# A decoder layer whose opening part is put in another order: weights and x turned first, one ternary form made by GpSimd, keys and values ahead of x1

## The chip, the cores and the metric

The kernel runs on one core of a Trainium2 chip, in one launch. The metric is the device time of that core in microseconds (us). In the text PE is TensorE, DVE is VectorE, ACT is ScalarE, POOL is GpSimd, SP is SyncE, which here only issues DMAs.

## The reference, cut to what matters

One post-norm decoder layer on 16 sequences of 256 tokens with 128 features, in three sub-layers, each followed by a residual sum and a layer norm.

```python
def bitlinear(x, weight):                       # weights made ternary
    scale = clip(mean(abs(weight), axis=1), 1e-05)
    w_q = clip(round(weight / scale), -1, 1)
    return x @ (weight + (w_q * scale - weight)).T

# 1: gated linear recurrence -> x1
r = sigmoid(bitlinear(x, Wr)); k = bitlinear(x, Wk); v = bitlinear(x, Wv)
scale = exp(positions * log(sigmoid(decay)))
state = cumsum(k * v / clip(scale, 1e-10)) * scale
x1 = layernorm(x + bitlinear(rmsnorm(r * state, ln_w), Wo))
# 2: cross attention, 16 heads of 64, over 1601 keys of ctx -> x2
q = x1 @ Wq + bq; k = ctx @ Wk + bk; v = ctx @ Wv + bv
x2 = layernorm(x1 + softmax(q k^T / 8) v @ Wo + bo)
# 3: top-1 mixture of 8 experts with capacity 512 -> output
x3 = layernorm(x2 + moe(x2))
```

## The kernel before, in words

Each engine has an instruction stream written out by hand, and semaphores tie the streams together. The attention goes by sequences ("batches" b, 16 of them) and within one by pairs of heads ("slots" s, 8 of them), 128 pairs in all. For each pair PE makes the keys (`keys`, lines 1406 to 1411, four pieces of 400 columns), the queries (`queries`, 1413), for every two pairs the values (`values`, 1424 to 1433, seven fills, 39 matmuls), then the row maxima of the scores (`maximum`, 1435, which DVE reduces at line 1048), the scores (`score_unit`), their sum with the exponentials from ACT (`attend`, 1473) and the denominators. Operands of keys, queries and values are split in a high part (`_hi`) and a low part (`_lo`), and each product is three matmuls, such as 1409, 1410 and 1411.

PSUM is a ring of eight banks. `all_fills` lists every fill of the ring in the order in which PE makes it, with the engine that empties it; all streams take bank numbers and semaphore counts from that list, so the list and the streams are changed together.

The recurrent sub-layer is done for two sequences at a time (a "step"). Step 0 stands in the prologue, ahead of the first batch. Its stages are: `step_tokens` (PE turns x), `step_rkv` (PE makes r, k and v with the ternary weights), `key_value`, `state`, `gated` (DVE, the chain that ends in `gain`), `step_products` (PE: the output product o and the sums of squares ss), `mean_square` (DVE), a power on POOL, `residual` and `step_moments` (DVE), another power on POOL, `normed` (DVE, writes `x1_rows`), `step_x1` (PE turns x1), and then high and low parts of x1, queries of pair 0 and its 16 maxima. From the maxima the `row_shift` of pair 0 goes through DRAM by SP's DMAs (`turn_shift`, 488 to 501) and comes back as `shift` (ACT, line 789); the first score matmul waits for it.

Before step 0 can start, DVE makes the ternary forms of four weights (lines 922 to 933), then the decay tables (936 to 948: a scan, a reciprocal, copies, memsets). PE in the meantime turns the context (`context`, line 1367), then the four ternary weights (`turn_weights`, 1344) and x. ACT copies three turned weights to `w_T`; DVE writes the fourth, scaled by ln_w (line 952), at the end of its tables, and `step_rkv` waits for it. POOL makes the low parts `wk_lo` (593) and `wv_lo` (605).

The staged copies of the projection weights (`wq_rows`, `wk_rows`, `wv_rows`) and the buffers of the ternary work lie in `v_sb`, which later holds the values, in two halves of 3328 columns per partition: the values of pairs 0 and 1 go in the first half. In the rows below all of these show as `v_sb`.

The order of PE in the prologue before is:

```python
for c in range(4): context(at, 0, c)
turn_weights(); step_tokens(at, 0)
pe.wait_ge(setup_ev_act, 1); pe.wait_ge(setup_ev_dve, 1)
step_rkv(at, 0); step_products(at, 0); context_read(at, 0)
pe.wait_ge(wk_split, 1)
for c in range(4): keys(at, 0, c)
step_x1(at, 0); pe.wait_ge(wq_split, 2); queries(at, 0)
# 16 maxima of pair 0, then seven value fills, keys and queries of pair 1, the bias row bo
```

Of the kernel before, what the change touches and what calls it, by code (L numbers as in the profile page):

```python
# [5 lines left out]
P = 128  # L6
F32 = mybir.dt.float32
# [3 lines left out]
ALU = mybir.AluOpType  # L11
ACT = mybir.ActivationFunctionType
# [20 lines left out]
V_FILLS = 7  # L33
# [38 lines left out]
def all_fills(batches):  # L72
# [3 lines left out]
    put = lambda owner, *key: fills.append((key, owner))  # L76
# [4 lines left out]

    for c in range(4):
        put("dve", "ctx", 0, c)
    step(0, "xt", "r", "kk", "vv", "o", "ss")
    for c in range(4):
        put("dve", "k", 0, c)
    step(0, "x1t")
# [4 lines left out]
    for n in range(V_FILLS):  # L92
        put("act", "v", 0, n)
# [105 lines left out]
def decoder_layer(nc, x, ctx, Wr, Wk, Wv, Wo, decay, ln_w, xWq, xbq, xWk, xbk, xWv, xbv, xWo, xbo,  # L199
                  fWr, fW1, fW2, out):  # L200
    B, T, D = x.shape
# [40 lines left out]
    with ExitStack() as stack:  # L242
# [3 lines left out]
        def sem(name):  # L246
            return stack.enter_context(nc.semaphore(name))
# [103 lines left out]
        wq_rows, wk_rows, wv_rows = (spare[:, n * AD:(n + 1) * AD] for n in range(3))  # L351
        w_rows, w_tmp, w_tern = (spare[:, 3 * AD + n * 4 * P:3 * AD + (n + 1) * 4 * P].rearrange("p (m n) -> p m n", n=P)
# [214 lines left out]
        def _(pool):  # L567
# [146 lines left out]
        def _(act):  # L714
# [202 lines left out]
        def _(dve):  # L917
# [7 lines left out]
            own(v.tensor_scalar(w_nhalf[:, :], w_scale[:, :], -0.5, None, ALU.mult))  # L925
# [319 lines left out]
            gated(at, 0)  # L1245
            dve.wait_ge(wq_in, 16)
# [3 lines left out]
            mean_square(at, 0)  # L1250
            dve.wait_ge(biases_in, 16 * 3)
            v.tensor_scalar(bq_s[:, :], bq_c[:, :], SCALE, None, ALU.mult).then_inc(wq_split, 1)
            residual(at, 0)
            step_moments(0)
            for c in range(4):
                keys_low(at, 0, c)
            normed(0)
# [77 lines left out]
        def _(pe):  # L1335
# [365 lines left out]
```

## Time and profile before

| | us |
|---|---|
| median of 3 runs | 2752.68 (2751.89 to 2753.65) |
| profiled execution, its own time | 2738.68 |
| span of its trace | 2736.9 |
| PE busy in it | 2670.3 (98%) |
| DVE busy | 2118.1 (77%) |
| POOL busy | 2152.7 (79%) |
| ACT busy | 1725.9 (63%) |

The span runs from the first to the last instruction of the trace. The profiled execution's time is 1.8 us longer than its span and 14.0 us shorter than the median of the runs; times below are read in the trace and carried over to the median as differences. Busy time of PE is taken with modelled ends of the matmuls.

### The profile page before, as it was taken

How to read it: one execution, taken by the hardware profiler on the slowest of the kernel's cores; microseconds unless marked ns; L12 is line 12 of the kernel's file. 1: busy time of each engine (PE TensorE's matmuls, PEld its weight loads, DVE VectorE, ACT ScalarE, POOL GpSimd, SP SyncE). 2: the span in 40 equal slices, each digit the busy share in tenths (PEclk: the TensorE clock that was granted, in tenths of full speed). 3: DMA queues.
4: the chain of work that ended last, by engine and by line, in shares of the span. 5: the costliest groups of instructions: out<-in, count | busy, mean ns of one | idle time of the engine just before them, and what ended most of it. 6: DMA issues, size and time to landing. Idle time of an engine off the chain costs nothing.

```text
span 2736.9 us, 70932 instructions
## 1 busy us (share of the span) xinstructions
PE 2670.3 (98%) x28456; PEld 2281.9 (83%) x28456; DVE 2118.1 (77%) x4293; ACT 1725.9 (63%) x3470; POOL 2152.7 (79%) x1749
## 2 busy tenths in 40 slices
PE   5999999999999999999999999999999999999977
PEld 4888888888888888888888888888888888888855
DVE  6677877788787887878778787878878878787744
ACT  3666666666666666766657666666666666666632
POOL 1778878888888877888878888888788887888845
PEclk7999999999999999999999999999999999999989
DMA  4000000000000000000000000000000000000030
GB/s 101 7 22 8 26 11 8 24 9 27 10 8 25 11 23 9 22 12 11 25 8 22 11 25 11 8 23 13 22 10 23 9 10 23 8 11 9 12 99 27
DMA packets 81099, 53.48 MB, mean 20 GB/s; under 512 B 14240, under 2 KB 78454, under 8 KB 80769
## 3 DMA queue, kind: packets, MB, share of 16 engines
q1 hardware_dynamic: 75600, 45.27, 6.1%
q8 instruction: 224, 3.67, 0.6%
q0 software_dynamic: 2048, 3.66, 0.4%
q14 instruction: 107, 0.87, 0.1%
q10 hardware_dynamic: 3120, 0.01, 0.1%
HBM read 40.76 MB, written 8.72 MB: 18 GB/s over the span
## 4 chain that ended last, share of the span: by engine, by line
PE 96%; DVE 1%; POOL 1%; ACT 1%; issue 0%; DMA 0%; SPq 0%; POOLq 0%; DVEq 0%; ACTq 0%
PE ps L1449 28%; PE ps L1480 26%; PE ps L1439 9%; PE ps L1430 4%; PE ps L1432 4%; PE ps L1431 4%; PE ps L1409 3%; PE ps L1411 3%; PE ps L1410 3%; PE ps L1496 3%; PE ps L1520 2%; PE ps L1651 1%; PE ps L1662 1%; PE ps L1385 1%; PE ps L1367 1%; PE ps L1422 1%
## 5 line engine op out<-in xcount | busy, mean ns | idle before, releaser
L622 POOL TENSOR_TENSOR key_sums<-key_sums,prob_T 65x512 f32<-65x512 f32 x1402 | 1816.4, 1296 | 161.7 <-POOL key_sums L622 1.8
L1048 DVE TENSOR_REDUCE mx<-ps 128x1 f32<-128x400 f32 (+1 forms) x2048 | 1057.3, 569 | 264.5 <-PE ps L1439 211.5
L818 ACT ACTIVATE prob_T<-ps 128x512 f32<-128x512 f32 x1536 | 834.1, 596 | 103.2 <-PE ps L1449 56.9
L1449 PE MATMUL ps<-shift,shift_w 64*128 64x256 f32 (+1 forms) x3328 | 765.9, 282 | 1.3 <-ACT shift L789 1.3
L1449 PE MATMUL ps<-q_hi,k_hi 64*128 64x256 f32 (+1 forms) x3328 | 758.9, 284 | 0.0
L1480 PE MATMUL ps<-prob_T,v_sb 128*64 128x256 f32 (+1 forms) x6656 | 740.5, 379 | 0.9 <-ACT prob_T L818 0.9
L1449 PE MATMUL ps<-q_lo,k_hi 64*128 64x256 f32 (+1 forms) x3328 | 737.6, 277 | 0.0
L1449 PE MATMUL ps<-q_hi,k_lo 64*128 64x256 f32 (+1 forms) x3328 | 736.6, 277 | 0.0
L1480 PEld LDWEIGHTS ps<-prob_T,v_sb 128*64 128x64 f32 (+1 forms) x6656 | 478.3, 137 | 241.5 <-ACT prob_T L818 1.8
L1449 PEld LDWEIGHTS ps<-shift,shift_w 64*128 64x128 f32 (+1 forms) x3328 | 570.0, 180 | 50.5 <-issue 50.3
L1449 PEld LDWEIGHTS ps<-q_hi,k_hi 64*128 64x128 f32 (+1 forms) x3328 | 544.7, 181 | 7.9 <-ACT prob_T L818 1.1
L1449 PEld LDWEIGHTS ps<-q_lo,k_hi 64*128 64x128 f32 (+1 forms) x3328 | 550.0, 181 | 0.0
L1449 PEld LDWEIGHTS ps<-q_hi,k_lo 64*128 64x128 f32 (+1 forms) x3328 | 548.9, 181 | 0.0
L1439 PE MATMUL ps<-k_hi,q_hi 64*128 64x400 f32 (+1 forms) x2048 | 532.0, 350 | 1.2 <-DVE q_lo L1039 1.2
L1033 DVE SCALAR_TENSOR_TENSOR k_lo<-ps,bk_c,k_hi 128x400 fp32r<-128x400 f32 (+1 forms) x512 | 317.4, 633 | 195.6 <-ACT k_hi L767 195.0
L618 POOL TENSOR_TENSOR key_sums<-prob_T 128x512 f32<-128x512 f32 x128 | 165.5, 1293 | 319.5 <-ACT prob_T L818 319.3
L1439 PEld LDWEIGHTS ps<-k_hi,q_hi 64*128 64x128 f32 x2048 | 329.5, 185 | 4.5 <-DVE mx L1048 1.5
L799 ACT COPY heads_raw<-ps 128x256 f32<-128x256 f32 x128 | 47.8, 373 | 409.9 <-PE ps L1480 370.0
L767 ACT ACTIVATE k_hi<-ps,bk_c 128x400 fp32r<-128x400 f32 (+1 forms) x512 | 302.2, 596 | 6.3 <-PE ps L1411 3.3
L783 ACT COPY v_sb<-ps 128x512 f32<-128x512 f32 x384 | 225.8, 588 | 53.6 <-PE ps L1432 8.9
L1430 PE MATMUL ps<-wv_hi,ctx_hi 128*128 128x256 f32 (+1 forms) x832 | 247.6, 298 | 0.0
L1079 DVE RECIPROCAL rden<-den 128x256 f32<-128x256 f32 x128 | 223.3, 1744 | 19.3 <-ACT den L794 17.9
(198 smaller groups left out, 3576.9 us busy)
## 6 DMA issues: line engine op xcount, KB each, us to landing
shift_f<-row_shifts SPq DMA_DIRECT2D x256, 64.0 KB, 2.6
ctx_raw<-in_ctx_dram SPq DMA_DIRECT2D x16, 768.0 KB
row_shifts<-nm_T SPq DMA_DIRECT2D x512, 0.5 KB
prob_T<-in_L_ffn_W_dram SPq DMA_DIRECT2D x12, 256.0 KB, 5.7
slots_in<-no_row SPq DMA_DIRECT2D x1, 2080.0 KB, 14.4
v_sb<-slots_in SPq DMA_DIRECT2D x8, 260.0 KB, 4.5
x_in<-in_x_dram SPq DMA_DIRECT2D x8, 256.0 KB, 2.9
out_dram<-x1s SPq DMA_DIRECT2D x16, 128.0 KB, 4.2
```

What stands on the lines that cost most here:

```text
L618: op = nc.gpsimd.tensor_tensor(acc[:, :, :], prob_T[:, :, 0, :], prob_T[:, :, 1, :], ALU.add)
L622: op = nc.gpsimd.tensor_tensor(acc[0:rows, :, :], acc[0:rows, :, :], prob_T[0:rows, :, k, :], ALU.add)
L767: nc.scalar.activation(k_hi[r % 2][:, KEY0[c]:KEY0[c] + WID[c]], ps[:, at.bank("k", r, c), 0:WID[c]], ACT.Identity, bias=bk_c[:, r % NJ:r ...
L783: copy(v_sb[:, g % 2, 2 * n:2 * n + 2, :], src).then_inc(ring_act, 1)
L818: nc.scalar.activation(prob_T[:, h, 2 * i - 2:2 * i, :].rearrange("p k t -> p (k t)"), ps[:, bank, :], ACT.Exp).then_inc(ring_act, 1)
L1033: v.scalar_tensor_tensor(k_lo[r % 2][:, cols], ps[:, at.bank("k", r, c), 0:WID[c]], bk_c[:, r % NJ:r % NJ + 1], k_hi[r % 2][:, cols].bitca ...
L1048: v.tensor_reduce(mx[:, qt, h, c:c + 1], ps[:, at.bank("mx", r, c, qt, h), 0:WID[c]], AX.X, ALU.max).then_inc(ring_dve, 1)
L1079: v.reciprocal(rden[:, :], den[:, :]).then_inc(rden_ok, 1)
L1430: mm(o, ctx_hi[:, cols], wv_hi[:, g0:g0 + 2 * P], start=True, stop=False)
L1439: mm(ps[:, bank, 0:WID[c]], q_hi[r % 2][lanes, qt * P:qt * P + P], k_hi[r % 2][lanes, KEY0[c]:KEY0[c] + WID[c]], start=True, stop=True).th ...
L1449: return mm(ps[0:rows, bank, n * T:n * T + T], keys_part, query_part[lanes, :], start=(step == 0), stop=(step == 3))
L1480: last = mm(ps[h * DH:h * DH + DH, bank, 0:T], v_sb[0:rows, r % NJ // 2 % 2, k, v0 + h * DH:v0 + h * DH + DH], prob_T[0:rows, h, k, :], st ...
```

## The change

PE turns the weights first, then x, then the context. The ternary form of the fourth weight (Wo) is made by POOL (six instructions of 128x128) instead of DVE (four), and its scaling by ln_w moves from DVE to ACT. POOL also clears the tables that DVE cleared with memsets; the scan takes its zeros from `key_sums[0]`. `wv_lo` on POOL comes ahead of the two powers, and `wv_hi` on ACT ahead of the gate. The values of the first two pairs are made between the keys of pair 0 and the turning of x1, instead of behind the maxima of pair 0. On DVE two of the four low parts of the keys come ahead of the residual sum, and `wq_lo` moves behind `normed`. The staged weights move to the end of `v_sb`, so that the first values can be written while they are still read.

```diff
 all_fills:
+    step(0, "xt")
     for c in range(4):
         put("dve", "ctx", 0, c)
-    step(0, "xt", "r", "kk", "vv", "o", "ss")
+    step(0, "r", "kk", "vv", "o", "ss")
     for c in range(4):
         put("dve", "k", 0, c)
+    for n in range(V_FILLS):
+        put("act", "v", 0, n)
     step(0, "x1t")
     ...
-    for n in range(V_FILLS):
-        put("act", "v", 0, n)
 GpSimd:
+            nc.gpsimd.memset(key_sums[0][:, :, :], 0.0).then_inc(tables_clear, 1)
+            nc.gpsimd.memset(carry[:, :, :], 1.0).then_inc(tables_clear, 1)
+            pool.wait_ge(tables_clear, 2)
+            nc.gpsimd.memset(carry[:, :, 0:1], 0.0).then_inc(tables_clear, 1)
+            nc.gpsimd.memset(scale_t[:, :, 0:1], 1.0).then_inc(tables_clear, 1)
+            pool.wait_ge(tern_in, 16 * 6)
+            pool.wait_ge(thresholds, 1)
+            own(nc.gpsimd.tensor_scalar(w_tmp[:, 3, :], w_rows[:, 3, :], w_half[:, 3:4], None, ALU.is_gt))
+            own(nc.gpsimd.tensor_scalar(w_tern[:, 3, :], w_rows[:, 3, :], w_nhalf[:, 3:4], None, ALU.is_lt))
+            own(nc.gpsimd.tensor_tensor(w_tern[:, 3, :], w_tern[:, 3, :], w_tmp[:, 3, :], ALU.subtract))
+            own(nc.gpsimd.tensor_scalar(w_tmp[:, 3, :], w_tern[:, 3, :], w_scale[:, 3:4], None, ALU.mult))
+            own(nc.gpsimd.tensor_tensor(w_tmp[:, 3, :], w_tmp[:, 3, :], w_rows[:, 3, :], ALU.add))
+            nc.gpsimd.tensor_tensor(w_tern[:, 3, :], w_rows[:, 3, :], w_tmp[:, 3, :], ALU.subtract).then_inc(tern_out, 1)
             (wk_lo as before)
+            pool.wait_ge(w_hi, 2)
+            nc.gpsimd.tensor_tensor(wv_lo[:, :], wv_rows, wv_hi[:, :].bitcast(F32), ALU.subtract).then_inc(wv_split, 1)
             step_rms(start, 0)
             step_rstd(0)
-            (wait and wv_lo, which stood here)
 ScalarE:
+            act.wait_ge(setup_tr, 1)
+            copy(w_T[:, 0:3, :], ps[:, 7, 0:3 * P].rearrange("p (m n) -> p m n", m=3)).then_inc(setup_ev_act, 1)
+            nc.scalar.activation(w_T[:, 3, :], ps[:, 7, 3 * P:4 * P], ACT.Copy, scale=lnw_c[:, :]).then_inc(setup_ev_act, 1)
+            tokens_in(at, 0)
             for c in range(4):
                 context_high(at, 0, c)
-            (the wait, the copy of w_T and tokens_in, which stood here)
-            gate_and_keys(at, 0)
             act.wait_ge(wv_in, 16)
             copy(wv_hi[:, :], wv_rows).then_inc(w_hi, 1)
+            gate_and_keys(at, 0)
     ...
             for c in range(4):
                 keys_high(at, 0, c)
+            for n in range(V_FILLS):
+                values_out(at, 0, n)
             x1T_out(at, 0)
 VectorE:
-            for m in range(4):
+            for m in range(3):
     ...
-            own(v.memset(carry[:, :, :], 0.0))
-            own(v.memset(scale_t[:, :, 0:1], 1.0))
+            dve.wait_ge(tables_clear, 4)
     ...
-            own(v.memset(carry[:, :, 1:T], 1.0))
-            dve.wait_ge(setup_tr, 1)
-            dve.wait_ge(setup_ev_act, 1)
-            v.tensor_scalar(w_T[:, 3, :], ps[:, 7, 3 * P:4 * P], lnw_c[:, :], None, ALU.mult)\
-                .then_inc(setup_ev_dve, 1)
     ...
             gated(at, 0)
+            mean_square(at, 0)
+            (bq_s as before)
+            for c in range(2):
+                keys_low(at, 0, c)
+            residual(at, 0)
+            step_moments(0)
+            for c in range(2, 4):
+                keys_low(at, 0, c)
+            normed(0)
             (wq_lo, which stood right behind gated)
             tokens_low(0)
 TensorE:
+            turn_weights()
+            step_tokens(at, 0)
             for c in range(4):
                 context(at, 0, c)
-            turn_weights()
-            step_tokens(at, 0)
-            pe.wait_ge(setup_ev_act, 1)
-            pe.wait_ge(setup_ev_dve, 1)
+            pe.wait_ge(setup_ev_act, 2)
             step_rkv(at, 0)
     ...
             for c in range(4):
                 keys(at, 0, c)
+            pe.wait_ge(wv_split, 1)
+            for n in range(V_FILLS):
+                values(at, 0, n)
             step_x1(at, 0)
     ...
-            pe.wait_ge(wv_split, 1)
-            for n in range(V_FILLS):
-                values(at, 0, n)
```

## Rows read from the trace of the kernel before

**Rows 1.** The chain that ended last, its shares of the span by engine.
```profile
PE 96%; DVE 1%; POOL 1%; ACT 1%; issue 0%; DMA 0%; SPq 0%; POOLq 0%; DVEq 0%; ACTq 0%
```

**Rows 2.** The chain's pieces in 0 to 80 us: start us, length us, engine, tile, line.
```profile
9.91 2.42 DVE v_sb L928
...
20.08 0.36 DVE w_T L952
20.53 4.85 PE ps L1385 x6
25.48 0.70 DVE kv L965
...
34.78 1.15 DVE work L994 x4
35.95 0.87 DVE stats_a L1001 x4
...
39.61 2.10 DVE x_rows L1012 x4
41.76 1.13 PE ps L1403 x4
...
46.69 5.40 PE ps L1439 x16
```

**Rows 3.** Waits of PE in 0 to 80 us.
```profile
PE ps L1385 <- DVE w_T L952: 5.1, 1, 5.1
```

**Rows 4.** Timeline, 9 to 20 us: start, length, engine, line, operation, tiles, shapes.
```profile
6.79 0.17 DVE L925 TENSOR_SCALAR w_nhalf<-w_scale 128x4 f32<-128x4 f32 x1
9.83 2.34 POOL L593 TENSOR_TENSOR wk_lo<-v_sb,wk_hi 128x1024 fp32r<-128x1024 f32 x1 [6.60 <-ACT wk_hi L722]
9.91 2.41 DVE L928 SCALAR_TENSOR_TENSOR v_sb<-v_sb,w_nhalf 128x128 f32<-128x128 f32 x1
11.48 2.90 PE L1367 MATMUL ps<-ident,ctx_raw 128*128 128x128 f32 x13 [11.48 <-DMA ctx_raw<-in_ctx_dram]
14.04 0.29 DVE L932 TENSOR_TENSOR v_sb<-v_sb 128x128 f32<-128x128 f32 x1
```

**Rows 5.** Groups by line and shape, POOL, whole span: busy us, mean ns.
```profile
L618 POOL TENSOR_TENSOR key_sums<-prob_T 128x512 f32<-128x512 f32 x128 | 165.5, 1293 | 319.5 <-ACT prob_T L818 319.3
L652 POOL TENSOR_SCALAR x1s<-x_rows,mv,rstd 128x128 f32<-128x128 f32 x32 | 25.2, 798 | 1.7
L584 POOL CAST tri_b<-tri 128x128 bf16<-128x128 f32 x1 | 0.3, 289 | 0.1
```

**Rows 6.** Timeline, DVE at 313 us and POOL at 306 us.
```profile
313.89 4.20 DVE L1012 TENSOR_SCALAR x_rows<-work,mv_a,rstd_a 128x128 f32<-128x128 f32 x4
...
306.85 15.27 POOL L622 TENSOR_TENSOR key_sums<-key_sums,prob_T 65x512 f32<-65x512 f32 x11
```

**Rows 7.** Stretches: PE, PEld, DVE, ACT, POOL busy us, PEclk, DMA, GB/s.
```profile
11.40:14.40 3.00, 2.92 (x14) 2.65 (x14) 2.82 (x8) 1.26 (x3) 0.78 (x1) 1.00 1.07 355
14.40:15.50 1.10, 1.08 (x8) 0.84 (x8) 0.80 (x3) 1.03 (x3) 0.00 (x0) 1.00 0.54 115
17.80:20.50 2.70, 0.00 (x0) 0.00 (x0) 2.40 (x5) 0.00 (x0) 0.00 (x0) 0.50 0.00 0
20.50:24.60 4.10, 4.07 (x5) 1.85 (x6) 2.12 (x6) 0.88 (x2) 0.00 (x0) 0.50 0.11 24
33.10:37.60 4.50, 4.42 (x13) 3.85 (x13) 2.95 (x17) 1.82 (x4) 1.12 (x2) 0.50 0.10 23
38.30:41.70 3.40, 0.00 (x0) 0.00 (x0) 3.40 (x7) 0.00 (x0) 2.55 (x2) 1.00 1.21 250
52.00:55.30 3.30, 3.30 (x16) 3.28 (x16) 3.30 (x9) 0.90 (x2) 0.00 (x0) 0.50 0.02 5
55.30:62.60 7.30, 7.30 (x57) 7.18 (x55) 2.96 (x7) 5.77 (x12) 0.00 (x0) 1.00 0.06 18
```

**Rows 8.** Timeline, 20 to 42 us: low parts, keys' high part, POOL beside normed.
```profile
20.79 1.96 DVE L1022 TENSOR_TENSOR ctx_lo<-ps,ctx_hi 128x512 fp32r<-128x512 f32 x4
35.56 0.59 ACT L767 ACTIVATE k_hi<-ps,bk_c 128x400 fp32r<-128x400 f32 x1 [0.34 <-PE ps L1411]
37.36 2.25 DVE L1033 SCALAR_TENSOR_TENSOR k_lo<-ps,bk_c,k_hi 128x400 fp32r<-128x400 f32 x4
38.51 2.34 POOL L605 TENSOR_TENSOR wv_lo<-v_sb,wv_hi 128x1024 fp32r<-128x1024 f32 x1
```

**Rows 9.** Timeline, PE at 52 and 56 us: value matmuls at half and full clock.
```profile
52.61 0.41 PE L1432 MATMUL ps<-wv_hi,ctx_lo 128*128 128x256 f32 x1
52.82 0.41 PE L1430 MATMUL ps<-wv_hi,ctx_hi 128*128 128x256 f32 x1
...
56.19 0.28 PE L1431 MATMUL ps<-wv_lo,ctx_hi 128*128 128x256 f32 x1
56.31 0.28 PE L1432 MATMUL ps<-wv_hi,ctx_lo 128*128 128x256 f32 x1
```

**Rows 10.** Timeline, 47 to 63 us: from the maxima to the first score.
```profile
47.39 7.80 DVE L1048 TENSOR_REDUCE mx<-ps 128x1 f32<-128x400 f32 x16 [0.85 <-PE ps L1439]
55.42 0.21 DVE L1061 STREAM_TRANSPOSE nm_T<-nm 128x32 f32<-128x32 f32 x1
58.19 0.35 PE L1409 MATMUL ps<-ctx_hi,wk_hi 128*128 128x400 f32 x1
61.42 0.40 ACT L789 CAST shift<-shift_f 128x256 fp32r<-128x256 f32 x1
60.73 1.95 PE L1624 MATMUL ps<-wo_rows,bv_c 128*128 128x128 f32 x16
62.60 0.33 PE L1449 MATMUL ps<-shift,shift_w 64*65 64x256 f32 x1
```

More of the change, by code:

```diff
@@ L350, in decoder_layer @@
         spare = v_sb[:, :, :, :].rearrange("p g k n -> p (g k n)")
-        wq_rows, wk_rows, wv_rows = (spare[:, n * AD:(n + 1) * AD] for n in range(3))
-        w_rows, w_tmp, w_tern = (spare[:, 3 * AD + n * 4 * P:3 * AD + (n + 1) * 4 * P].rearrange("p (m n) -> p m n", n=P)
+        STAGED = KT * 2 * P
+        wq_rows, wk_rows, wv_rows = (spare[:, STAGED + n * AD:STAGED + (n + 1) * AD] for n in range(3))
+        w_rows, w_tmp, w_tern = (spare[:, n * 4 * P:(n + 1) * 4 * P].rearrange("p (m n) -> p m n", n=P)
                                  for n in range(3))
@@ L385, in decoder_layer @@
         tern_ready = sem("tern_ready")
+        tern_out = sem("tern_out")
         decay_exp = sem("decay_exp")
@@ L388, in decoder_layer @@
         setup_ev_act = sem("setup_ev_act")
-        setup_ev_dve = sem("setup_ev_dve")
+        thresholds = sem("thresholds")
+        tables_clear = sem("tables_clear")
         w_hi = sem("w_hi")
@@ L600, in step_rstd @@
                 power(rstd_a[:, :], ve_a[:, :], a_var, i + 1, a_pow)
+            pool.wait_ge(w_hi, 2)
+            nc.gpsimd.tensor_tensor(wv_lo[:, :], wv_rows, wv_hi[:, :].bitcast(F32), ALU.subtract).then_inc(wv_split, 1)
             step_rms(start, 0)
             step_rstd(0)
-            pool.wait_ge(w_hi, 2)
-            nc.gpsimd.tensor_tensor(wv_lo[:, :], wv_rows, wv_hi[:, :].bitcast(F32), ALU.subtract).then_inc(wv_split, 1)
             def sum_keys(at, s):
@@ L866, in _ @@
             at = start
+            act.wait_ge(setup_tr, 1)
+            copy(w_T[:, 0:3, :], ps[:, 7, 0:3 * P].rearrange("p (m n) -> p m n", m=3)).then_inc(setup_ev_act, 1)
+            nc.scalar.activation(w_T[:, 3, :], ps[:, 7, 3 * P:4 * P], ACT.Copy, scale=lnw_c[:, :]).then_inc(setup_ev_act, 1)
+            tokens_in(at, 0)
             for c in range(4):
                 context_high(at, 0, c)
-            act.wait_ge(setup_tr, 1)
-            copy(w_T[:, 0:3, :], ps[:, 7, 0:3 * P].rearrange("p (m n) -> p m n", m=3)).then_inc(setup_ev_act, 1)
-            tokens_in(at, 0)
-            gate_and_keys(at, 0)
             act.wait_ge(wv_in, 16)
             copy(wv_hi[:, :], wv_rows).then_inc(w_hi, 1)
+            gate_and_keys(at, 0)
             act.wait_ge(wq_in, 16)
@@ L884, in _ @@
             queries_high(at, 0)
-            for n in range(V_FILLS):
-                values_out(at, 0, n)
             for c in range(4):
@@ L924, in _ @@
             own(v.tensor_scalar(w_half[:, :], w_scale[:, :], 0.5, None, ALU.mult))
-            own(v.tensor_scalar(w_nhalf[:, :], w_scale[:, :], -0.5, None, ALU.mult))
-            for m in range(4):
+            v.tensor_scalar(w_nhalf[:, :], w_scale[:, :], -0.5, None, ALU.mult).then_inc(thresholds, 1)
+            dve.wait_ge(thresholds, 1)
+            for m in range(3):
                 own(v.tensor_scalar(w_tmp[:, m, :], w_rows[:, m, :], w_half[:, m:m + 1], None, ALU.is_gt))
@@ L938, in _ @@
             own(v.tensor_scalar(dec[:, 3:4], dec[:, 2:3], 1e-7, None, ALU.max))
-            own(v.memset(carry[:, :, :], 0.0))
-            own(v.memset(scale_t[:, :, 0:1], 1.0))
-            own(v.tensor_tensor_scan(scale_t[:, 0, 1:T], dec[:, 3:4].broadcast_to([P, T - 1]), carry[:, 0, 1:T],
+            dve.wait_ge(tables_clear, 4)
+            own(v.tensor_tensor_scan(scale_t[:, 0, 1:T], dec[:, 3:4].broadcast_to([P, T - 1]), key_sums[0][:, 0, 1:T],
                                      1.0, ALU.mult, ALU.add))
@@ L1245, in _ @@
             gated(at, 0)
+            mean_square(at, 0)
+            dve.wait_ge(biases_in, 16 * 3)
+            v.tensor_scalar(bq_s[:, :], bq_c[:, :], SCALE, None, ALU.mult).then_inc(wq_split, 1)
+            for c in range(2):
[5 more added lines that the diff above has]
+            normed(0)
             dve.wait_ge(wq_in, 16)
@@ L1249, in _ @@
                 .then_inc(wq_split, 1)
[L1250 to L1257, printed above, removed]
             tokens_low(0)
@@ L1340, in turn_weights @@
             def turn_weights():
-                pe.wait_ge(tern_ready, 4)
+                pe.wait_ge(tern_ready, 3)
+                pe.wait_ge(tern_out, 1)
                 for m in range(4):
@@ L1614, in _ @@
                 maximum(at, 0, *unit, 0)
-            pe.wait_ge(wv_split, 1)
-            for n in range(V_FILLS):
-                values(at, 0, n)
             for c in range(4):
```

## The prediction, made before the result was known

> **What bounds the kernel now.** I read the chain of waits first. By engine it is 96% PE [rows 1]: from the first score matmul on, nothing but PE's own work decides, so an edit of the prologue is worth what it takes off the moment of that first matmul, 62.60 us [rows 10], and nothing more. Then I read the pieces of the chain in the prologue: there it runs through other engines, DVE's ternary work and tables up to 20.4, r, k and v on PE (20.53 to 25.38), DVE, PE, POOL and DVE again up to the turning of x1 at 41.76, and the maxima from 46.69 [rows 2]. Third the waits of PE: 5.1 us of idle before r, k and v, released by DVE's line 952 [rows 3]. Fourth the timeline and the granted clock by stretches: PE works at half clock in most of the prologue, and at full clock from 55.3 on [rows 7]. At the first score, PE itself was last: the shift was ready at 61.42 + 0.40 = 61.82, PE finished the bias row at about 62.6 [rows 10].
>
> **The front: weights, tables, r, k, v.** Before, the last ternary form was ready at 14.33 and `step_rkv` waited for 20.43 [rows 2, 4]. Now PE waits neither for the tables nor for line 952, only for the ternary forms, the turning and ACT's copies. The question is when the forms are there. The thresholds stand at 6.96 [rows 4]. POOL's three tensor_tensor of 128x128: a line through 512 elements in 1.293 us and 1024 in 2.34 us gives 0.51 each [rows 4, 5]. Its three one-operation tensor_scalar are in no row; the nearest are the cast (0.29) and the two-operation form (0.80) [rows 5]; I take 0.55. With gaps of 0.1, the difference between the 1.39 us cadence and the 1.29 us duration in [rows 5, 6], that is 3.8 us, if POOL waits for nobody. But DVE and POOL get in each other's way: one DVE instruction that takes 0.35 elsewhere took 2.41 when POOL's `wk_lo` had begun 0.08 us earlier [rows 4], and in the main loop four small DVE instructions took 4.20 us beside a row of POOL's, about one for each of POOL's [rows 6]. So I let the two engines take turns: POOL's six end at about 11.3, DVE has then done seven of its twelve, one more gets in before `wk_lo` (11.4 to 13.7), and the last four at 0.32 end at 15.0. Bounds: 13.0, if only `wk_lo` blocks, at its old place (12.3 plus two instructions), to 17.0, if nothing overlaps (POOL 3 x 0.51 + 3 x 0.80, `wk_lo` 2.34, DVE 12 x 0.32). I take 15.0, so PE starts 3.5 us later than now (11.48).
>
> The Trainium skill, "SBUF — State Buffer", section "SBUF: two separate sides", says that VectorE and GpSimd share one pair of ports as an exclusive lock, held for the whole instruction, against GpSimd instructions that read SBUF and VectorE ones with two SBUF inputs or in a two-port mode. The trace agrees (0.35 us became 2.41 us). By that rule alone the forms would come at the late bound, 17.0.
>
> From 15.0: the eight transposes of weights and x at 0.21 each (the 13 of the context took 2.90, a tail of 0.2 included [rows 4]) are 1.7 us, the context's 13 another 2.7 at that rate. Before, the clock was granted in full by 2.9 us (11.48 to 14.4) in one case and 4.1 us (20.5 to 24.6) in another after PE began to work [rows 7]; here that is about 18.5, so the context ends at about 19.1 and r, k and v take half of 4.85, 2.4 plus a tail of 0.2: v at 21.7. ACT (three copies 1.4 us, four high parts 2.4, `wv_hi` 1.05) ends at 21 and then gate and keys' copies keep step. DVE is later: its tables took 14.3 to 20.4; without two memsets of 0.5, a small one, their gaps and line 952 (1.6 together) 4.6, then memsets 0.4 and `ctx_lo` 1.96 [rows 8]: 15.0 + 7.0 = 22.0. So `kv` starts at 22.0 instead of 25.48, -3.5. `wv_lo` now runs at about 21.1 to 23.4 and holds up the second product (two SBUF inputs, like the instruction of [rows 4]) by 0.6. Sum of the front: -2.9. Bounds: -5.4 (forms at 13.0) and +0.4 (forms at 17.0 with PE at half clock all the way: 17.0 + 4.5 + 4.85 = 26.3, less 0.5 for the tail).
>
> **x1.** `wv_lo` held `normed` back: its four instructions took 2.10 instead of about 1.15 [rows 2, 8]. That stall goes. But two `keys_low` now stand ahead of the residual, and the second waits for `k_hi` of piece 1, ready at 36.15 in old times; with 0.6 each DVE is free at 36.8, where the residual stood at 34.78: +2.0. The other two `keys_low` hide beside POOL's power. In old times: residual 36.8, moments to 39.4, power to 40.65, `normed` to 41.85, against 41.71: +0.1. Bounds -1.4 (keys at full clock) to +1.0. `wq_lo`, 1.2 us, moves to a place where DVE waits over 2 us for PE and ACT: nothing.
>
> **Values ahead of x1.** In new times the rows of x1 are ready at 41.8 - 2.9 = 38.9. PE ends the keys at 34.6 (37.5 before) and has 39 value matmuls: 0.118 each at full clock, 4.6 us, or 0.213 at half clock, 8.3 us [rows 9]. Before, full clock came at 38.3, 5.2 us after the keys began at 33.1 [rows 7]; the same here is 35.4. 0.8 us at half and the rest at full: 39.5, so x1 is turned 0.6 late: +0.6. Bounds 0 and +4.0. With the clock up, turning x1 and the queries are 0.6 shorter (0.36 + 0.3; bounds 0 and 0.8): -0.6. The 16 maxima stay bound by DVE at 0.485 each [rows 10].
>
> **To the first score.** The values are gone from behind the maxima; there remain keys, queries and bias row of pair 1, 4.5 us at full clock (58.19 to 62.7) and about 8.5 at half, beginning 3 us before the last maximum is read. The shift takes 6.7 us from the last maximum (55.1 to 61.82) [rows 10], so the shift, not PE, is last in either case: 61.82 in old times instead of 62.60: -0.75 (bounds 0 and -0.8).
>
> **The clock at the first score.** Sum so far: -2.9 + 0.1 + 0.6 - 0.6 - 0.75 = -3.55, first score at 59.05. But before, PE came to it straight from 10 us of dense work, at full clock. Now it idles 1 to 4.5 us there. After 5 us of idle the clock was half at 20.5 and stayed so for 4.1 us of work, which costs 2.05 us [rows 7]. In PE-bound work that is paid in full. I take +2.0; bounds 0 and +4.3 (half of the 8.6 us from 46.7 to 55.3). Then -1.55: profiled span 2736.9 to about 2735.4, own time 2738.68 to 2737.1. The median is 14.0 us above the profiled time; the difference carries over: 2752.68 - 1.55 = 2751.1. The sum of all the bounds is -9.8 to +9.0; they won't all fall together.
>
> SP's DMAs of the second context, x and the zeroed slots are issued where they were, within 3 us; the zeroing (14.4 us to landing) ended before the shift's DMAs and still does.
>
> **The rivals.** (a) As the sum, but the clock stays up at the first score: 2752.68 - 3.55 = 2749.1. For it: PE works on for 6 of the 9 us behind the maxima. Against it: at 17.8 the clock was down 2.3 us after PE fell idle [rows 7]. (b) The forms come at 13.0, POOL and DVE hardly meeting, and the clock stays up: front -5.4, so -6.05: 2746.6. For it: no row shows how long a POOL instruction as small as 128x128 keeps DVE off. Against it: [rows 6]. (c) The lock is complete, forms at 17.0: DVE's tables then end the front at 24.0 with 0.1 of the other stall, front -1.4: -1.55 + 1.5 = -0.05: 2752.6. For it: [rows 4, 6]; against it: DVE got its turns between POOL's instructions in [rows 6] without POOL's cadence growing. (d) Slower: the values run at half clock ahead of x1. Place: PE between keys and `step_x1`; price 8.3 us of values against 4.3 us of cover, +4.0 instead of +0.6, and the 0.6 of faster turning lost: +2.4 to 2.5 over the time before, 2755.1. It decides from the point where full clock comes more than about 2.5 us after the keys end. For it: 4.5 us of keys ended at half clock in [rows 7]; against it: the clock was full 0.7 us later.
>
> **How the numbers follow.** Forecast 0.47, (a) 0.20, (b) 0.13, (c) 0.10, (d) 0.10. About 0.2%, 5.5 us, is what a measurement of this kernel can tell from no change. Only (b) and the early edge of (a) are beyond it on the fast side: 0.14. On the slow side it takes (d) and (c) together: 0.04. Within: 0.82. The likeliest one's own range is 2749 to 2753; the whole range takes in (a), (c), (d) and most of (b): 2745.5 to 2756.0.
>
> **What would show it.** PE's first transposes at 15.0 and of weights; DVE's ternary instructions stretched to 0.7 us and more while POOL works; `kv` at 22.0; residual about 2 us behind the mean square's power; values at 34.6 to 39.5 with the clock rising in them; a PE idle of over 1 us released by `shift` before the first score, at 59.05; half clock for some 4 us behind it. It would be wrong if the forms came after 17, if x1's turning came later than 41.8, if the first score were not where the whole span's difference (less the clock's cost) arose, or if the main loop itself changed in length.

## The result, and the profile after

| | before | after |
|---|---|---|
| median of 20 runs each | 2752.68 (2751.89 to 2754.43) | 2749.2 (2747.61 to 2750.24) |
| ratio, 95% interval | | 0.9986 (0.998 to 0.9993) |
| first score matmul, us from the start of the trace | 62.60 | 57.60 |
| first product with the values (52 matmuls of line 1480, now 1499) | 76.40 | 72.95 |
| span of the traced execution | 2736.9 | 2748.2 |

The changed kernel is 3.5 us faster, 0.14%: inside the 0.2% that counts here as no change, but its interval lies clear of 1. The forecast was 1.55 us faster. Below, "first score" is the first score matmul of PE, and "first attend" the first product with the values; both are read in a trace.

The waits of PE in the first 75 us of the changed kernel (waited for: us in total, times, longest) answer to [rows 3]:

```profile
PE ps L1363 <- DVE v_sb L955: 13.6, 1, 13.6
PE ps L1410 <- DVE gain L996: 4.8, 1, 4.8
PE ps L1468 <- ACT shift L810: 3.1, 1, 3.1
```

The wait for line 952 is gone. PE now waits for the last ternary form, which is its first work, and a new wait of 3.1 us stands right before the first score, released by the shift: what followed the maxima on PE was moved away, as forecast. The front in the timeline of the changed kernel, to be held against [rows 4]:

```profile
7.02 0.62 POOL L606 TENSOR_SCALAR v_sb<-v_sb,w_half 128x128 f32<-128x128 f32 x1 [2.64 <-DVE w_nhalf L947]
7.18 0.35 DVE L951 SCALAR_TENSOR_TENSOR v_sb<-v_sb,w_nhalf 128x128 f32<-128x128 f32 x1
8.48 0.46 POOL L608 TENSOR_TENSOR v_sb<-v_sb 128x128 f32<-128x128 f32 x1
8.53 0.56 DVE L951 SCALAR_TENSOR_TENSOR v_sb<-v_sb,w_nhalf 128x128 f32<-128x128 f32 x1
9.04 0.62 POOL L609 TENSOR_SCALAR v_sb<-v_sb,w_scale 128x128 f32<-128x128 f32 x1
9.12 0.43 DVE L953 SCALAR_TENSOR_TENSOR v_sb<-v_sb,w_scale 128x128 f32<-128x128 f32 x1
10.27 0.46 POOL L611 TENSOR_TENSOR v_sb<-v_sb 128x128 f32<-128x128 f32 x1
10.31 0.56 DVE L951 SCALAR_TENSOR_TENSOR v_sb<-v_sb,w_nhalf 128x128 f32<-128x128 f32 x1
10.68 2.39 POOL L614 TENSOR_TENSOR wk_lo<-v_sb,wk_hi 128x1024 fp32r<-128x1024 f32 x1
10.91 2.31 DVE L953 SCALAR_TENSOR_TENSOR v_sb<-v_sb,w_scale 128x128 f32<-128x128 f32 x1
13.25 0.29 DVE L955 TENSOR_TENSOR v_sb<-v_sb 128x128 f32<-128x128 f32 x1
15.38 2.87 PE L1386 MATMUL ps<-ident,ctx_raw 128*128 128x128 f32 x13
18.05 2.82 PE L1404 MATMUL ps<-work,w_T 128*128 128x512 f32 x6
20.98 0.69 DVE L981 TENSOR_TENSOR kv<-kv,ps 128x512 f32<-128x512 f32 x1 [0.74 <-PE ps L1404]
21.70 1.11 DVE L984 TENSOR_TENSOR kv<-kv,tables 128x512 f32<-128x512 f32 x1
```

Beside POOL's small instructions DVE's grow from 0.35 to 0.56 at most; beside the long `wk_lo` the 0.35 becomes 2.31, as before. The stall of [rows 4] was not removed, only met by another instruction. How much DVE loses goes with POOL's operation and not with its length. An instruction of DVE's forms that met one of POOL's two-input tensor_tensor ended 0.08 to 0.15 us after it, whether that was short or long: POOL's ended at 8.94, 10.19, 10.73 and 13.07, DVE's at 9.09, 10.27, 10.87 and 13.22. Beside POOL's one-input tensor_scalar (lines 606, 607 and 609) DVE's took 0.35, 0.34 and 0.43 where they take 0.35, 0.29 and 0.35 alone. `wv_lo` costs 0.42 at line 984. Further on, the turning of x1 and the way to the first score:

```profile
36.45 1.12 DVE L1028 TENSOR_SCALAR x_rows<-work,mv_a,rstd_a 128x128 f32<-128x128 f32 x4
38.70 0.60 PE L1422 MATMUL ps<-ident,x_rows 128*128 128x128 f32 x4
43.43 7.80 DVE L1064 TENSOR_REDUCE mx<-ps 128x1 f32<-128x400 f32 x16 [0.85 <-PE ps L1458]
52.59 1.95 PE L1642 MATMUL ps<-wo_rows,bv_c 128*128 128x128 f32 x16
57.06 0.40 ACT L810 CAST shift<-shift_f 128x256 fp32r<-128x256 f32 x1 [3.66 <-DMA shift_f<-row_shifts]
57.60 0.30 PE L1468 MATMUL ps<-shift,shift_w 64*65 64x256 f32 x1 [3.06 <-ACT shift L810]
```

The rows of x1 are ready at 37.57, x1 is turned at 38.70, when PE has ended the values: 1.1 us late. PE's bias row ends at 54.5 and the shift is ready at 57.46. The same in stretches of the changed kernel (columns as in [rows 7]):

```profile
13.60:18.00 4.40, 4.35 (x21) 4.38 (x22) 4.01 (x10) 2.51 (x5) 0.00 (x0) 1.00 0.32 75
18.10:20.90 2.80, 2.77 (x8) 0.99 (x6) 2.05 (x6) 2.72 (x6) 0.99 (x1) 1.00 0.00 0
29.10:33.10 4.00, 4.00 (x13) 3.96 (x14) 1.87 (x6) 1.78 (x3) 1.06 (x1) 0.50 0.00 0
33.20:38.70 5.50, 5.50 (x40) 5.50 (x40) 5.33 (x20) 3.68 (x7) 1.01 (x1) 0.82 0.70 177
54.40:57.50 3.10, 0.14 (x2) 0.00 (x0) 0.29 (x1) 0.40 (x1) 0.00 (x0) 1.00 0.13 42
59.00:62.40 3.40, 3.40 (x35) 3.40 (x33) 2.23 (x5) 1.81 (x4) 1.46 (x2) 0.51 0.02 5
```

r, k and v ran at 2.4 GHz (a granted share of 1.00), the keys at 1.2 GHz (0.50), the values at a mix. In the front of a trace the granted share can't be trusted: it reads 1.00 from 13.60 to 18.00 too, where the 13 transposes of the context took 2.87, some 0.21 us apart, which is half pace (at full pace those of x stand 0.11 apart in the first trace of before). Up to the first fall that is recorded, PE's pace has to be read from the distance of its matmuls. Here it doubled at 18.0. After 3.1 us of idle the clock fell at 59.1, in the middle of the scores, for 3.4 us: 35 matmuls where 59 fit at full clock (below). Of 5.00 us won at the first score 1.55 are lost again by the first attend: 76.40 - 72.95 = 3.45, against 3.48 in the medians. That they agree so closely is luck, since the kernel before, traced again (below), had its first attend at 76.13.

**Why the spans say the opposite.** By the traced executions the changed kernel is 11.3 us longer. From the first attend to the end of the span, before took 2660.5 us and after 2675.2: 14.7 us more in a part that the change does not touch. It comes mostly in steps of 0.8 and 1.3 us, in turn, at the first pair of each sequence from the fourth on. Such a place in the timeline, of the kernel before and then of the changed one:

```profile
707.00 0.97 POOL L664 DMA_INDIRECT slots_in<-x_rows,dest  x1 [0.30 <-issue]
706.07 6.38 ACT L818 ACTIVATE prob_T<-ps 128x512 f32<-128x512 f32 x11 [0.45 <-PE ps L1449]
```

```profile
704.94 0.97 POOL L685 DMA_INDIRECT slots_in<-x_rows,dest  x1 [0.30 <-issue]
706.42 1.54 DVE L1064 TENSOR_REDUCE mx<-ps 128x1 f32<-128x400 f32 x3 [1.24 <-PE ps L1458]
706.44 1.08 ACT L839 ACTIVATE prob_T<-ps 128x512 f32<-128x512 f32 x2 [1.34 <-PE ps L1458]
```

In the changed kernel's trace ACT and DVE both stand still for 1.3 us beside the scatter of the previous sequence's rows (`DMA_INDIRECT`), with finished scores in front of them; in the other one nothing happens at the same place. The question was whether the change brought these stalls. It did not: see the kernel before run again, below.

### The profile page after: what moved, and what is told of

The parts are those of the page before. It is cut to its first block, busy times and chain, and to the rows that moved or that the text cites. A ratio compares the mean times of both kernels' runs of the same rounds, so it can differ in the third digit from the quotient of the medians.

```text
span 2748.2 us, 70936 instructions
## 1 busy us (share of the span) xinstructions
PE 2678.9 (97%) x28456; PEld 2285.3 (83%) x28456; DVE 2113.6 (77%) x4285; ACT 1724.7 (63%) x3471; POOL 2158.8 (79%) x1759
## 4 chain that ended last, share of the span: by engine, by line
PE 95%; DVE 1%; POOL 1%; issue 1%; DMA 1%; ACT 1%; SPq 0%; POOLq 0%; DVEq 0%; ACTq 0%
PE ps L1468 28%; PE ps L1499 26%; PE ps L1458 9%; PE ps L1449 4%; PE ps L1451 4%; PE ps L1450 4%; PE ps L1428 3%; PE ps L1430 3%; PE ps L1429 3%; PE ps L1515 3%; PE ps L1539 2%; POOL out_dram L715 1%; PE ps L1386 1%; PE ps L1404 1%; PE ps L1441 1%
## 5 line engine op out<-in xcount | busy, mean ns | idle before, releaser
L1095 DVE RECIPROCAL rden<-den 128x256 f32<-128x256 f32 x128 | 223.3, 1744 | 19.3 <-ACT den L815 17.9
```

What stands on the lines that cost most here:

```text
L1095: v.reciprocal(rden[:, :], den[:, :]).then_inc(rden_ok, 1)
```

## The experiments

All were timed beside runs of the kernel before; ratio and interval are against those. "Forms turned" is the start of PE's first transpose of a ternary form, "kv" that of DVE's first product of k and v, "x1 turned" the start of `step_x1`; all are read in one trace of each kernel. "Won" is how far the median lies under that of the kernel before in the same group of runs, in us. The runs came in three groups, in which the kernel before had medians of 2753.07 (e1, e2, e3, e4), 2751.1 (e3b, e5, e6, e10) and 2738.63 (e9, e11, e12 and the kernel before again).

| | forms turned | kv | x1 turned | first score | first attend | won | ratio (95%) |
|---|---|---|---|---|---|---|---|
| before | 14.38 | 25.48 | 41.76 | 62.60 | 76.40 |  |  |
| before_again | 14.66 | 25.27 | 41.55 | 62.36 | 76.13 | -0.25 | 1.0002 (0.9992, 1.0012) |
| changed | 13.65 | 20.98 | 38.70 | 57.60 | 72.95 | 3.5 | 0.9986 (0.998, 0.9993) |
| e1_front_only | 13.71 | 21.49 | 37.68 | 59.40 | 73.21 | 3.7 | 0.9986 (0.9977, 0.9995) |
| e4_values_behind | 13.79 | 21.28 | 37.76 | 59.23 | 73.03 | 3.5 | 0.9987 (0.9978, 0.9996) |
| e6_residual_first | 13.86 | 21.77 | 37.89 | 56.48 | 71.78 | 3.3 | 0.9988 (0.9979, 0.9997) |
| e3_pe_kept_busy | 13.83 | 20.88 | 38.50 | 58.64 | 72.43 | 4.9 | 0.9983 (0.9974, 0.9992) |
| e3b_filler_half | 13.74 | 20.95 | 38.64 | 57.55 | 71.35 | 5.2 | 0.9979 (0.997, 0.9988) |
| e2_low_parts_late | 12.02 | 20.06 | 36.16 | 54.80 | 70.12 | 6.2 | 0.9977 (0.9968, 0.9986) |
| e5_forms_on_dve | 12.44 | 20.29 | 36.38 | 55.02 | 70.33 | 4.8 | 0.9982 (0.9973, 0.9991) |
| e10_split_values | 11.64 | 19.65 | 34.55 | 53.42 | 67.31 | 8.2 | 0.9969 (0.9957, 0.9981) |
| e11_values_in_gaps | 11.79 | 19.38 | 33.67 | 52.32 | 66.21 | 8.9 | 0.9966 (0.9954, 0.9978) |
| e9_wk_behind_forms | 11.96 | 22.45 | 39.42 | 58.34 | 73.63 | 1.9 | one run |
| e12_before_wk_late | 14.29 | 23.21 | 39.50 | 60.57 | 74.36 | 2.5 | 0.9991 (0.9982, 1.0) |

Most intervals reach some 2.5 us to either side. Where the text tells kernels apart by 1 to 2 us, it rests on the traces and not on the times.

**The front alone, and the values put back.** e1 takes only the front of the change into the kernel before; e4 takes the values out of the changed one:

```diff
-            pe.wait_ge(wv_split, 1)
-            for n in range(V_FILLS):
-                values(at, 0, n)
             step_x1(at, 0)
     ...
                 maximum(at, 0, *unit, 0)
+            pe.wait_ge(wv_split, 1)
+            for n in range(V_FILLS):
+                values(at, 0, n)
     (the same move on ScalarE and in all_fills)
```

> The kernel before with the front of the change alone (weights and x turned first, the fourth ternary form on POOL, tables cleared by POOL, the scaled copy on ACT); values stay behind the maxima, wv_lo behind the powers, keys_low and wq_lo where they were. Theory A, the front is the whole gain and moving the values buys nothing, because PE comes to the first score at full clock when the values lie right before it: kv starts at about 21.0, first score at 62.6 - 4.5 = 58.1 at full clock, first attend at about 71.9 (72.95 with the whole change), time 4.5 us under before, 1 under the whole change. Rival B, the values' move carries its 0.75 us and more: first attend at 73.7 or later, time 2.7 us or less under before.

> The changed kernel with the values of the first pairs put back behind the maxima, the rest of the change kept. Theory A, the move gains 0.75 us at the shift and loses 1.7 us by the clock: x1 is turned at about 37.6 instead of 38.7, first score at 58 to 58.5 at full clock, first attend at 71.5 to 72.2, time 1 us under the changed kernel. Rival B, the move is worth what it gains at the shift: time 0.8 us or more over the changed kernel.

Measured: 3.7 and 3.5 us under before, as the whole change (3.5). So the front is all of the net gain, and the move of the values buys nothing. Both theories had the sizes wrong. e1 fell between its two: first score at 59.40 and first attend at 73.21, not 58.1 and 71.9. In e4 the first score comes 1.6 us later than in the changed kernel, not 0.5 to 1, and in exchange PE comes to it at full clock:

```profile
49.00:52.60 3.60, 3.60 (x19) 3.60 (x18) 2.60 (x8) 1.51 (x3) 0.00 (x0) 0.50 0.02 5
52.80:59.20 6.40, 6.40 (x50) 6.30 (x48) 2.67 (x5) 4.98 (x11) 0.00 (x0) 1.00 0.07 21
59.20:62.40 3.20, 3.20 (x50) 3.17 (x51) 2.81 (x7) 1.94 (x5) 0.16 (x1) 1.00 0.00 0
```

In those 3.2 us of e4 PE starts 50 matmuls, in the same stretch of the changed kernel 35 in 3.4. The 1.6 us won at the shift and the 1.55 us lost by the clock cancel.

**The clock at the first score.** More products, whose results are overwritten, fill PE's wait for the shift:

```diff
             bank = bank_of(at, "bo", 0)
+            for j in range(10):      # 20 in e3
+                mm(ps[:, bank, 0:P], bv_c[:, j % NJ:j % NJ + 1].broadcast_to([P, P]), wo_rows[:, j % NJ, :], start=True, stop=True)
```

> The changed kernel with 20 more 128x128 products (results overwritten) ahead of the bias row, 2.4 us at full clock, in the 3.1 us in which PE waits for the shift. Theory A, that idle lets the clock fall behind the first score: the same first score at 57.5, then no half clock from 59.1 to 62.5, first attend 1.7 us earlier at about 71.2, time 1.7 us under the changed kernel. Rival B, the fall comes from something else (the sparse maxima before): half clock stays, time unchanged.

> As e3_pe_kept_busy with 10 extra products instead of 20: there each product was two matmuls in the trace, 4.6 us for 40, so PE itself came 1.1 us late to the first score (58.64). Theory A: PE ends at about 56.6, first score at 57.5 by the shift, clock full from there on, first attend at 71.3 against 72.95 in the changed kernel, time 1.6 us under it. Rival B: a wait of 1 us is enough for the clock to fall: half clock for 3.4 us after the first score, time as the changed kernel.

With 20 the fall of the clock was gone, but the filler was mis-sized: each product is two matmuls in the trace, and PE came to the score 1.0 us late. With 10 (timeline and stretch of e3b):

```profile
54.71 1.95 PE L1644 MATMUL ps<-wo_rows,bv_c 128*128 128x128 f32 x16
57.55 0.30 PE L1468 MATMUL ps<-shift,shift_w 64*65 64x256 f32 x1 [0.88 <-ACT shift L810]
59.00:62.40 3.40, 3.40 (x59) 3.40 (x58) 3.26 (x8) 2.92 (x6) 1.69 (x2) 1.00 0.02 7
```

The first score stands where it stood, the first attend is 1.60 us earlier than in the changed kernel, and its ratio to before is 0.9979 against 0.9986 (the intervals overlap). All the traces say the same: where PE idled 3.1 to 3.5 us before the first score (changed, e2, e5, e6, e9), the first attend came 15.3 us behind it; where it idled 1.1 us or less (all the others), 13.8 to 13.9. That PE's idleness costs 1.5 us there, and useless work wins it back, is shown by the traces.

**POOL's long instructions.** e2 holds the two long POOL instructions back to where DVE works from PSUM or waits:

```diff
+            pool.wait_ge(ring_dve, start.freed("ctx", 0, 0)[1])
             pool.wait_ge(w_hi, 1)        # wk_lo
...
+            pool.wait_ge(a_y, 1)
             pool.wait_ge(w_hi, 2)        # wv_lo
```

> The changed kernel with wk_lo held back until DVE reads the context's first low part, and wv_lo until DVE has made the gain. Theory A, the shared ports cost 2.3 us at DVE's line 953 and 0.4 us at line 984: forms ready at 11.3 instead of 13.55, kv at 18.4 to 18.8 instead of 20.98, its second product 0.69 instead of 1.11, first score at 54.8 to 55.1 instead of 57.5, time 2.5 us (1 to 3.5, by how the clock falls) under the changed kernel. Rival B, the context's arrival at 11.4 and PE's half clock hold the front instead: kv not before 20.0, time within 1 us of the changed kernel.

Measured: the forms at 11.92, kv at 20.06, its second product 0.69, first score 54.80, 2.8 us earlier than in the changed kernel at both marks. kv came 1.3 us later than theory A allowed: PE was the last there (DVE waited 1.44 us for it), because its pace doubled only at 17.9, 6 us after its first work, and all the transposes and the first part of r, k and v ran at half pace. In that theory A was wrong, and rival B's "not before 20.0" came true; but the time is theory A's. e9 moves `wk_lo` only behind the forms:

> The changed kernel with wk_lo waiting only for DVE's last form. Theory A: the forms come at about 11.9 as in e2_low_parts_late, but wk_lo then meets the small instructions and the scan of the decay tables, one of which takes about 2.3 us longer; DVE reaches the context's low parts at 18.3 as in the changed kernel, and kv at 20.5 instead of 20.06. Rival B: the tables' small operands don't contend, and kv comes at 20.06 as in e2_low_parts_late.

Its timeline shows what such a long instruction does wherever it is put, if DVE has SBUF work:

```profile
11.93 2.35 POOL L615 TENSOR_TENSOR wk_lo<-v_sb,wk_hi 128x1024 fp32r<-128x1024 f32 x1 [0.94 <-DVE v_sb L956]
12.15 0.15 DVE L962 TENSOR_SCALAR dec<-dec 128x1 f32<-128x1 f32 x1
12.34 2.50 DVE L964 TENSOR_TENSOR_SCAN tables<-dec,key_sums 128x255 f32<-128x255 f32 x1
17.62 2.35 POOL L625 TENSOR_TENSOR wv_lo<-v_sb,wv_hi 128x1024 fp32r<-128x1024 f32 x1 [3.33 <-ACT wv_hi L896]
17.64 2.48 DVE L970 COPY tables<-tables 128x256 f32<-128x256 f32 x1
```

The scan takes 2.50 instead of 0.69, the copy 2.48 instead of 0.29; of DVE's work on SBUF only the instructions with one element per partition pass. kv comes at 22.45, later than in the changed kernel: neither theory had seen that `wv_lo`, too, would be met by the tables. e12 puts the one line of `wk_lo` into the kernel before:

> The kernel before with one line more: wk_lo waits until DVE reads the first context low part (about 20 us). Theory A, the shared ports: DVE's line 928 takes 0.35 instead of 2.41, forms ready at 12.3, tables and the scaled copy 2.1 us earlier, so PE starts r, k and v at 18.5 and the first score comes at 60.5 at full clock, time 2.1 us under before. wk_lo, at about 18.8 to 21.1, is in time for the keys at 31. Rival B, the stall only moves onto another DVE instruction with SBUF operands: time within 0.5 us of before.

```profile
11.71 0.35 DVE L931 SCALAR_TENSOR_TENSOR v_sb<-v_sb,w_scale 128x128 f32<-128x128 f32 x1
18.60 4.51 PE L1386 MATMUL ps<-work,w_T 128*128 128x512 f32 x6 [2.44 <-DVE w_T L953]
```

No instruction of DVE is stretched ahead of r, k and v (`wv_lo` still holds up `normed` later, 2.17 us for its four), r, k and v begin at 18.60 instead of 20.53, the first attend is 2.0 us earlier (1.8 against before_again, of the same group) and the median 2.5 us under before, with an interval that just reaches 1. One wait is worth between a half and some 0.7 of the whole change.

e5 is e2 with all four forms on DVE:

> As e2_low_parts_late, with all four ternary forms made by DVE and none by POOL. Theory A, the shared ports eat POOL's share: without POOL beside it DVE needs 1.3 us for a form, so four end at about 7.0 + 5.3 = 12.3, against 11.9 for three of them beside POOL: PE's first transpose 0.4 us later, time 0.4 us over e2_low_parts_late at most. Rival B, POOL's form saves a form's 1.3 us: time 1.3 us over it.

PE's first transposes come at 12.44 instead of 12.02, the first attend 0.2 us later. POOL's form, six instructions, saves DVE four of together 1.3 us and is worth 0.4 at that place, since DVE's other twelve take 4.73 us in e2 and 3.98 in e5. By the times e5 won 4.8 us and e2 6.2, a difference of 1.4 that is nearer to rival B; they ran in different groups and their intervals overlap, so the times settle nothing between 0.4 and 1.3, and the traces speak for theory A.

**Residual first.**

```diff
-            for c in range(2):
-                keys_low(at, 0, c)
             residual(at, 0)
             step_moments(0)
-            for c in range(2, 4):
+            for c in range(4):
                 keys_low(at, 0, c)
```

> The changed kernel with the residual and the moments ahead of all four keys_low on DVE. Theory A, PE's values hide it: the rows of x1 are ready at about 36 instead of 37.5, but PE ends the values at 38.6 in both and turns x1 at 38.7, time unchanged within 0.3 us. Rival B, DVE's order sets x1: x1 turned 1.5 us earlier and time 1.5 us less.

The rows of x1 were ready at 36.71, and PE turned it at 37.89, when it had ended the values: theory A's cover holds. Yet the turning came 0.8 us earlier than in the changed kernel, although kv was 0.8 us later. The stretch of the values in e6 tells why:

```profile
28.90:32.90 4.00, 4.00 (x14) 3.96 (x14) 2.24 (x10) 1.46 (x3) 1.06 (x1) 0.50 0.01 2
33.10:37.90 4.80, 4.80 (x42) 4.80 (x41) 4.71 (x14) 3.82 (x8) 1.01 (x1) 1.00 1.07 242
```

Here the clock rose at 33.1, in the changed kernel's trace at 35.2. Where it steps differs from one execution to the next even of one kernel: in the first trace of before PE turned x at full pace (four transposes in 0.60 us), in before_again at half pace (1.06). In the six traces with this front the rise at the values stands at 32.2 to 33.1 in three and at 34.8 to 35.2 in three. That moves a mark by about 1 us, so single traces of these kernels can't be compared to less than that, unless the mark stands ahead of PE's work. By the timed runs e6 (0.9988) and the changed kernel (0.9986) are the same; that the order of DVE here is worth nothing while PE makes the values is as far as it goes.

**Both together.** e10 has the late low parts, the residual first, and three of the value fills ahead of x1 and four behind the maxima; e11 puts one of the four into PE's wait behind the turning of x1, and two `keys_low` into DVE's wait for the queries.

> Low parts late, residual ahead of keys_low, and the seven value fills split: three ahead of x1, four behind the maxima. Theory A: x1 is turned when its rows are ready, at about 33.5 (37.0 in e2_low_parts_late, 38.7 in the changed kernel), the first score comes at 52 to 53.5 with the clock up because the four fills keep PE at work until about then, first attend at 66 to 67.5, time 5 to 6.5 us under the changed kernel and 2.5 to 4 under e2_low_parts_late. Rival B, PE at half clock needs 3 us more for the fills behind the maxima and comes last: first score at 54.5 or later, time within 1 us of e2_low_parts_late.

> As e10_split_values, with three value fills ahead of x1, one in PE's wait behind the turning of x1, three behind the maxima, and the last two keys_low moved into DVE's wait for the queries. Theory A: x1 is turned about 0.9 us earlier, the first score comes at about 52.5 by the shift, with at most 1 us of idle before it and the clock up, first attend at 66.4, time 0.9 us under e10_split_values. Rival B: PE with its fills and bias row at half clock comes last at 53.4 as there, time unchanged.

In e11, from the rise of the clock, behind PE's maxima, to the first scores:

```profile
47.50:51.20 3.70, 3.70 (x28) 3.55 (x26) 2.75 (x5) 2.53 (x5) 0.00 (x0) 1.00 0.11 34
51.20:52.30 1.10, 0.05 (x1) 0.01 (x1) 0.29 (x1) 0.41 (x1) 0.00 (x0) 1.00 0.02 6
52.30:58.00 5.70, 5.68 (x88) 5.70 (x90) 4.76 (x10) 4.25 (x9) 2.42 (x2) 1.00 0.01 4
```

The fills cover all but 1.1 us of the shift, the clock stays up, and x1 waits 0.1 us for PE instead of 1.1. e10 runs at 0.9969 and e11 at 0.9966 of before (0.9954 to 0.9978), 8.9 us faster where the whole change brought 3.5 (0.998 to 0.9993). It beats both kernels; e10 and e11 are not told apart by their times. e10's turning of x1 came 1 us later than expected, because four `keys_low` stood before `normed`; e11 mended that.

**The kernel before, again.**

> The kernel before, unchanged, traced once more. Its first trace took 2660.5 us from the first attend (76.40) to the end of the span; the changed kernel and the eight experiments took 2673.4 to 2675.3. Theory A, that first trace is the odd one and the main loop's extra stalls (0.8 to 1.3 us at the first pair of each sequence from the third on) belong to the kernel before as well: first attend at 76.4 again, span near 2750, the same stalls. Rival B, the change lengthened the main loop by 14 us: span again near 2737, and then the timed difference would need another cause.

Its span was 2736.8, its first attend stood at 76.13, and it had none of the stalls: by that alone, rival B. But in the same group every run of the kernel before took 2737 to 2741, and the kernels built on the changed one have no stalls there either. e9, the changed kernel with one wait more, took 2661.3 us from the first attend on and e11 2660.4, as the kernel before (2660.5 and 2660.7), where the changed kernel and the eight traces of the first two groups took 2673.4 to 2675.3. So the 14 us come with the group of runs and not with a kernel, and they don't come with the chip either, for the last two groups ran on the same one. Theory A was right that the change didn't bring them; its span near 2750 did not come. The first trace of before was indeed odd against its own timed runs: it has no stalls and took 2738.68, while none of the twenty took under 2751.89, which accounts for the 14.0 us between the trace and the median. What brings the stalls is open.

## Why the prediction was right

The sign, the places and the kind of each step were right; the sum was 1.9 us too small, more than half of what was measured. The front was 1.2 us of that, the clock 0.45, turning x1 with the queries 0.3, the shift 0.25, the rows of x1 0.1, and the values went 0.5 the other way. The range, 10.5 us wide, takes in no change as well, so the time alone says little for the forecast; the terms say more.

- Forms ready: forecast 15.0, measured 13.54. This is the term that was mis-sized. The two engines took turns, as in [rows 6], only at POOL's three tensor_tensor; its three tensor_scalar hardly held DVE up. So DVE's twelve had nine done and the tenth under way when `wk_lo` came, not eight, and the rest of the difference is POOL's end (10.73 instead of 11.3). POOL's one-operation tensor_scalar took 0.62 to 0.68 (0.55 taken), its tensor_tensor 0.46 (0.51). Rival (c), the full lock at 17.0, is out as a whole, though the three short tensor_tensor did hold DVE to their end; (b)'s 13.0, with only `wk_lo` blocking, was nearer for the forms than the forecast was.
- kv: 20.98 instead of 22.0. PE's pace doubled 4.4 us after its first work (2.9 and 4.1 in the rows of before), so r, k and v took 2.82 (2.6). `wv_lo` cost 0.42 (0.6). The forecast had DVE come last; DVE was free at 20.24 and waited 0.74 us for PE. The gain was ready at 25.60 against 29.68: -4.1 for the front instead of -2.9, inside its bounds.
- x1 rows: residual 2.1 us behind the power (2 forecast); rows ready 4.1 us earlier than before, so +0.0 (+0.1).
- Values ahead of x1: +1.1 instead of +0.6, since the clock rose 1.9 us into them and not 0.8. Rival (d) was this mechanism and needed 2.5 us.
- Turning x1, queries: 4.93 from x1's turning to the maxima became 4.03, -0.9 (-0.6).
- To the first score: 15.91 from the maxima's start became 14.87, -1.0 (-0.75); the shift was last.
- The sum to the first score is -5.0 (-3.55); the clock took 1.55 back (2.0), -3.45 (-1.55). The move of the values therefore won what it should at the shift and lost it by the clock. e4 shows the balance as nought, e3b the lost 1.6 by itself; rival (a), the clock staying up, is what e3b made of it. The measured 2749.2 lies on rival (a)'s 2749.1, but by luck: its mechanism did not occur, and the front made up for the clock.
- Carrying the difference over to the median held (3.45 in the trace, 3.5 in the medians), but not by comparing spans, as I had meant to: those differed by 11.3 us the other way. So two of the signs of being wrong did appear in the traces (a main loop of another length, a span whose difference arose elsewhere); e9, e11 and before_again show that they don't belong to the change.
- One sum of the prediction is wrong, though nothing hangs on it: its bounds add up to -8.4 and +9.7, not -9.8 and +9.0.

## What to carry to other kernels

Before moving elementwise work to GpSimd, look at what VectorE does meanwhile: here GpSimd's long two-input instruction cost VectorE what was left of its length wherever VectorE had work on SBUF, and the waits that put it beside PSUM work or idleness were worth 1.8 to 2.8 us in the traces, where the whole change brought 3.5. When TensorE's work is taken out from in front of a wait, price the clock after the idle stretch; leave enough of it there to fill the wait. And compare two traces mark by mark, not by their spans, before you believe a difference of half a per cent; better still, trace both kernels in the same group of runs.

## What the runs showed of the hardware

- VectorE's instructions on one PSUM and one SBUF operand ran at their usual length beside GpSimd's long tensor_tensor (the four context low parts 1.96 beside `wk_lo` in e2, as without it in [rows 8]; 0.69 at line 981 beside `wv_lo` in the changed kernel), and those with one element per partition did too (0.15 and 0.16 in e9). A scan, a copy and a scalar_tensor_tensor on SBUF alone waited for its end (2.50, 2.48, 2.31).
- The same held for short ones: beside GpSimd's 128x128 tensor_tensor of 0.46 us VectorE's 128x128 instruction ended 0.08 to 0.15 us after it in the changed kernel, e1, e2, e9 and e10. Beside GpSimd's one-input tensor_scalar of 0.62 to 0.68 us it took 0.34 to 0.43 instead of 0.29 to 0.35. Why the two differ is open.
- GpSimd's 128x128 fp32 tensor_scalar with a per-partition scalar (two comparisons and a product) took 0.62 to 0.68 us beside VectorE's work, more than its 128x128 tensor_tensor (0.45 to 0.46). How long it takes alone no run shows.
- After 3.1 us of idle the clock fell to 1.2 GHz not at once but 1.5 us after work had begun again, and stayed there for 3.4 us of dense work; in e2, e5, e6 and e9, with 3.3 to 3.5 us of idle, it fell 0.5 to 1.0 us after. With 0.6 us (e10), 0.9 us (e3b) and 1.1 us (e11) of idle it did not fall.
- The granted share reads 1.00 at the front of every trace, also where PE worked at half pace: in before_again r, k and v took 4.72 us (2.82 in the changed kernel) under a share of 1.00.
- In each of the three groups of runs the four traces agree, whatever the kernel: either all have stalls of ACT and DVE beside GpSimd's indirect DMAs, some 14 us in all, or none has. The times of the runs without a trace fit that (the kernel before at 2749.4 and over in the first two groups, at 2741.1 and under in the last).
